# A spiking stage and a linear attention merged into one program by half batches, in a two-layer hybrid kernel

## The reference

```
x = x + attention16(ln(x))       # stage 0, causal, 16 heads, low-rank keys and values
x = x + spiking(ln(x))           # stage 1
x = x + scan(ln(x))              # stage 2, selective scan, with its own rms norm
x = x + spiking(ln(x))           # stage 3, the weights of stage 1
x = x + linear_attention(ln(x))  # stage 4, normalized again, gamma and beta
x = x + experts(ln(x))           # stage 5, 8 experts, all for every token
x = x + attention16b(ln(x))      # stage 6
x = x + experts(ln(x))           # stage 7, the weights of stage 5
```

## Time and profile before

| what | value |
|---|---|
| median of 3 runs | 2260.16 us (2257.64 to 2265.5) |
| the profiled execution | 2259.06 us, of it span 2257.3 |
| mean granted TensorE clock | 0.924 |
| busy: TensorE, VectorE, ScalarE, GpSimd | 1870.5, 1676.5, 1115.6, 1023.6 us |

### The profile page before, as it was taken

The page is one execution under the profiler, slowest core; times in us unless marked ns, Lnnn a source line. Parts: engine busy times, 40 slices in busy tenths (PEclk is TensorE's granted clock), DMA queues, the critical chain, the costliest instruction groups (busy, mean ns, idle before and its releaser), DMA issues.

```text
span 2257.3 us, 32350 instructions
## 1 busy us (share of the span) xinstructions
PE 1870.5 (83%) x12288; PEld 1208.3 (54%) x12288; DVE 1676.5 (74%) x2145; ACT 1115.6 (49%) x1846; POOL 1023.6 (45%) x386
## 2 busy tenths in 40 slices
PE   6988989854888885559999987878887777899999
PEld 5444454343444444446777765555554545577776
DVE  4665555345799995536677779999999999977666
ACT  2344445421634321105555556666676666555554
POOL 3476766511177760110000018878898889700000
PEclk8898999886899997759999999989999999999999
DMA  2112111000200000011000000000000000000000
GB/s 71 29 31 56 29 29 30 1 10 11 38 1 0 1 0 10 5 32 45 27 29 15 15 1 1 1 1 1 2 1 22 9 1 1 29 29 29 15 15 19
DMA packets 35679, 39.12 MB, mean 17 GB/s; under 512 B 5891, under 2 KB 22534, under 8 KB 35526
## 3 DMA queue, kind: packets, MB, share of 16 engines
q1 hardware_dynamic: 34998, 36.01, 6.4%
q10 hardware_dynamic: 528, 1.05, 0.2%
HBM read 21.05 MB, written 1.05 MB: 10 GB/s over the span
## 4 chain that ended last, share of the span: by engine, by line
PE 43%; issue 18%; DVE 18%; POOL 13%; ACT 4%; SPq 2%; DMA 1%; DVEq 0%; POOLq 0%; ACTq 0%; PEldq 0%
PE ps L46 9%; PE ps L48 7%; PE ps L47 7%; DVE negm L2241 6%; POOL AF L698 4%; POOL hc L1332 3%; POOL AF L1332 3%; PE ps L502 2%; PE ps L486 2%; PE ps L527 2%; POOL AR_plain L2051 1%; PE ps L2075 1%; DVE AF L2248 1%; PE ps L2158 1%; PE ps L866 1%
## 5 line engine op out<-in xcount | busy, mean ns | idle before, releaser
L2241 DVE TENSOR_REDUCE negm<-ps 128x64 bf16<-128x1024 f32 x256 | 302.2, 1215 | 14.5 <-PE ps L2149 14.3
L698 POOL TENSOR_TENSOR AF<-AF 128x2048 f32<-128x2048 f32 (+3 forms) x73 | 234.2, 3208 | 154.6 <-ACT AF L638 148.6
L46 PE MATMUL ps<-XH,AR 128*128 128x512 f32 x616 | 257.2, 418 | 36.4 <-DVE AF L907 18.0
L2051 POOL TENSOR_TENSOR AR_plain<-AF 128x2048 f32<-128x2048 f32 x64 | 261.9, 4093 | 35.6 <-ACT AF L2199 34.7
L2207 ACT ACTIVATE AF<-ps 128x1024 f32<-128x1024 f32 x192 | 196.5, 1023 | 144.5 <-PE ps L2158 143.0
L48 PE MATMUL ps<-XH,AR 128*128 128x512 f32 x616 | 247.5, 402 | 0.0
L47 PE MATMUL ps<-XL,AR 128*128 128x512 f32 x616 | 246.9, 401 | 0.0
L2158 PE MATMUL ps<-negm,ident_bf 128*128 128x512 bf16 x512 | 162.4, 400 | 90.0 <-DVE negm L2241 89.9
L638 ACT ACTIVATE AF<-ps 128x512 f32<-128x512 f32 (+1 forms) x304 | 155.5, 576 | 148.3 <-PE ps L489 86.6
L2248 DVE TENSOR_REDUCE AF<-AF 128x128 f32<-128x2048 f32 x96 | 218.6, 2277 | 0.5 <-ACT AF L2207 0.5
L46 PEld LDWEIGHTS ps<-XH,AR 128*128 128x128 f32 x616 | 119.2, 194 | 78.5 <-DVE AF L907 22.5
(11 more groups left out here) (323 smaller groups left out, 4298.0 us busy)
## 6 DMA issues: line engine op xcount, KB each, us to landing
AR<-AR SPq DMA_DIRECT2D x96, 128.0 KB, 2.4
AF<-in_L_ffn_Wg_dram SPq DMA_DIRECT2D x21, 256.0 KB, 2.6
AF<-in_L_ffn_Wu_dram SPq DMA_DIRECT2D x21, 256.0 KB, 3.1
AF<-in_L_ffn_Wd_dram SPq DMA_DIRECT2D x21, 256.0 KB, 3.7
AF<-AF SPq DMA_DIRECT2D x16, 64.0 KB, 2.4
AF<-AR_plain SPq DMA_DIRECT2D x16, 64.0 KB, 2.4
AF<-in_L_attn_a_Wq_dram SPq DMA_DIRECT2D x1, 512.0 KB, 4.2
AF<-in_L_attn_a_Wout_dram SPq DMA_DIRECT2D x1, 512.0 KB, 8.9
```

The lines of the kernel that those rows point to most:

```text
L46: pe.matmul(out, ah, bh, start=start, stop=False)
L698: pool.tensor_tensor(zacc[u % 2][:, :, c0:512], zacc[u % 2][:, :, c0:512], pt[t % 4][:, :, 0:w], ALU.add).then_inc(s0_zp, 1)
L2051: pool.tensor_tensor(p6[m % 3].rearrange("p (j q i) -> p j q i", j=HJ, i=2), e6[m % 4].rearrange("p (j q i) -> p j q i", j=HJ, i=2), w6i[: ...
L2241: dve.tensor_reduce(negm6[:, j % 4, :], bank(2 * (j % 3), 2).rearrange("p (j q i) -> p q j i", j=HJ, i=2), mybir.AxisListType.XY, ALU.max, ...
```

## The change

Four things are done together.

1. **Early weights.** The spiking weights are fetched into `lnt`, a buffer that the norms of stages 2 and 4 use: for stage 1 at the very start of the kernel, for stage 3 once the norm of stage 2 is done. The scan's weights are fetched at the start of stage 1 and transposed ahead of its last `down`, the linear attention's at the start of stage 3, and the first two expert loads stand right behind them on SP.
2. **Heads of stages 1 and 3** by halves and quarters: statistics first, then the first half's norm, its two quarters, and the first up units before the other half.
3. **One program for stages 3 and 4** (`s34_*`). Once the second quarter's spikes are added, batch 0 is normed and its linear attention follows the spiking stage's last quarters in the order written out below. It ends with the norm for the experts of batch 0's two quarters alone.
4. **Guests.** Batch 1's linear attention and its norm for the experts (`s4_end_*`) stand between expert units 0 to 30; the expert units 0 to 31 use batch 0 only. The split of the fourth expert load moves from unit 18 to 20. The scan's buffers and those of stages 3 and 4 lie at other places of the arenas; `s4_*` is cut into one function per step; the addition of the result goes in two parts.

```diff
+        def fc_load(q, k):
+            q.dma_start(FC[k]["fc_raw"], a["L0_ffn_W_fc"]...).then_inc(s1_w, 16)
+            q.dma_start(FC[k]["pj_raw"], a["L0_ffn_W_proj"]).then_inc(s1_w, 16)
         def s1_load(q, s):
             q.wait_ge(x_done, X_AFTER[s])
-            q.dma_start(wfc_raw, ...); q.dma_start(wpj_raw, ...)
+            s2_load_weights(q)
+        def fc_head_pe(pe, s, between=None):
+            k = s // 2
+            fc_weights_pe(pe, k)
+            for i in (0, 1):
+                ln_quarter_pe(pe, s, i, bank(i))
+            fc_up(pe, k, 0)
+            for i in (2, 3):
+                pe.wait_ge(ln_lo, 4 * s + i - 1)
+                ln_quarter_pe(pe, s, i, bank(i - 2))
+            fc_up(pe, k, 1)
+        def fc_norm_dve(dve, link, s):
+            for h in range(2):
+                ln_tiles_stats(dve, link, range(HB * h, HB * h + HB))
+                ln_half_aggr(dve, link, h)
+            ln_tiles_norm(dve, s, range(0, HB))
+        def fc_head_dve(dve, s):
+            for i in (0, 1):
+                ln_quarter_dve(dve, s, i, bank(i))
+            ln_tiles_norm(dve, s, range(HB, NB))
+            fc_squares(dve, k, 0)
+            for i in (2, 3):
+                ln_quarter_dve(dve, s, i, bank(i - 2))
+            fc_squares(dve, k, 1)
...
+            # s1_pe
+            fc_down(pe, 0, 2)
+            s2_weights_pe(pe)
+            fc_down(pe, 0, 3)
...
+        def s34_load(q, s):
+            q.wait_ge(ln_lo, 4 * 2 + 4)
+            fc_load(q, 1)
+            q.wait_ge(x_done, X_AFTER[s])
+            s4_load(q)
+        def s34_pe(pe, s):
+            fc_head_pe(pe, s)
+            s4_weight_pe(pe)
+            fc_down(pe, 1, 0)
+            fc_up(pe, 1, 2)
+            fc_down(pe, 1, 1)
+            fc_up(pe, 1, 3)
+            fc_down(pe, 1, 2)
+            for i in (0, 1):
+                ln_quarter_pe(pe, 4, i, bank(i))
+            fc_down(pe, 1, 3)
+            s4_keys_pe(pe, 0, 6)
+            s4_values_pe(pe, 0, 0)
+            s4_transpose_pe(pe, 0, 6)
+            s4_context_pe(pe, 0, bank(2)[:, 0:P])
+            s4_out_pe(pe, 0, bank(3)[:, 0:P])
+            s4_fold_pe(pe, 0, bank(2)[:, 0:P])
+            pe.wait_ge(s1_yc, 8)
+            for i in (2, 3):
+                ln_quarter_pe(pe, 4, i, bank(2 + i))
+            for p in range(2):
+                s4_result_pe(pe, 0, p, bank(6 + p))
+            for i in (0, 1):
+                ln_quarter_pe(pe, 5, i, bank(i))
+        def s34_dve(dve, link, s):
+            fc_norm_dve(dve, link, s)
+            fc_weights_dve(dve, 1)
+            fc_head_dve(dve, s)
+            fc_spikes(dve, link, 1, 0)
+            fc_squares(dve, 1, 2)
+            fc_spikes(dve, link, 1, 1)
+            dve.wait_ge(x_done, X_AFTER[3] + 2)
+            ln_tiles_stats(dve, link, range(0, HB))
+            ln_half_aggr(dve, link, 0)
+            fc_squares(dve, 1, 3)
+            ln_half_center(dve, link, 4, 0)
+            ln_half_rescale(dve, link, 4, 0)
+            fc_spikes(dve, link, 1, 2)
+            s4_weights_dve(dve)
+            for i in (0, 1):
+                ln_gained_dve(dve, 4, i)
+            fc_spikes(dve, link, 1, 3)
+            s4_max_dve(dve, 0, bank(6, 2))
+            dve.wait_ge(x_done, X_AFTER[4])
+            ln_tiles_stats(dve, link, range(HB, NB))
+            ln_half_aggr(dve, link, 1)
+            s4_sum_dve(dve, link, 0)
+            s4_keys_dve(dve, 0, bank(6, 2))
+            ln_half_center(dve, link, 4, 1)
+            s4_mask_dve(dve, 0, bank(2)[:, 0:P])
+            s4_scale_dve(dve, 0, bank(3)[:, 0:P])
+            ln_half_rescale(dve, link, 4, 1)
+            s4_fold_dve(dve, 0, bank(2)[:, 0:P])
+            for i in (2, 3):
+                ln_gained_dve(dve, 4, i)
+            for p in range(2):
+                s4_add_dve(dve, link, 0, p, bank(6 + p))
+            dve.wait_ge(x_done, X_AFTER[4] + 1)
+            ln_tiles_stats(dve, link, range(0, HB))
+            ln_half_aggr(dve, link, 0)
+            moe_split_dve(dve, 0, 0)
+            ln_tiles_norm(dve, 5, range(0, HB))
+            for i in (0, 1):
+                ln_quarter_dve(dve, 5, i, bank(i))
...
+        END_TR = {27: 2, 28: 3}
+        def s4_end_pe(pe, n):      # called behind down_e(n)
+            if n == 0:
+                s4_keys_pe(pe, 1, 4)
+            if n == 4:
+                s4_values_pe(pe, 1, 4)
+            if n == 7:
+                s4_transpose_pe(pe, 1, 4)
+            if n == 10:
+                s4_context_pe(pe, 1, bank(4)[:, 0:P])
+            if n == 13:
+                s4_out_pe(pe, 1, bank(5)[:, 0:P])
+            if n == 15:
+                s4_fold_pe(pe, 1, bank(4)[:, 0:P])
+            if n in (17, 18):
+                s4_result_pe(pe, 1, n - 17, bank(4 + n - 17))
+            if n in END_TR:
+                ln_quarter_pe(pe, 5, END_TR[n], bank(2 + END_TR[n]))
```

```diff
         def moe_load(q, s):
-            if s == 5:
-                q.wait_ge(x_done, X_AFTER[s])
...
-                if s == 5 and l == 1:
+                if s == 5 and l == 3:
+                    q.wait_ge(x_done, X_AFTER[4])
                     s6_load(q)
```

More of the change, by code:

```diff
@@ new lines, in fc_up @@
+        def fc_up(pe, k, i):
+            for c in range(FF):
+                n = 16 * k + 4 * i + c
+                if i == 0 and c < 2:
+                    pe.wait_ge(s1_flo, k + 1)
+                    pe.wait_ge(s1_fpj, k + 1)
+                pe.wait_ge(ln_lo, 4 * (2 * k + 1) + i + 1)
+                wait(pe, s1_h, n - 1)
+                mm3(pe, bank(2 + n % 2), (FC[k]["hi"][:, P * c:P * c + P], FC[k]["lo"][:, P * c:P * c + P]),
+                    xt(512 * i, 512)).then_inc(s1_z, 1)
@@ new lines, in s4_sum_dve, with s4_transpose_pe @@
+        def s4_sum_dve(dve, link, b):
+            dve.wait_ge(s4_e, b + 1)
+            link(dve.reciprocal(k4r[:, b:b + 1], k4s[:, b:b + 1]))
+        def s4_transpose_pe(pe, b, first):
+            pe.wait_ge(s4_e, b + 1)
+            if b:
+                pe.wait_ge(s4_vc, b + 1)
+            for t in range(LB):
+                ins = pe.transpose(bank(first + t // 4)[:, P * (t % 4):P * (t % 4) + P], k4e[:, P * t:P * t + P],
+                                   ident[:, :])
+            ins.then_inc(s4_kt, 1)
@@ new lines, in s4_fold_dve, with s4_result_pe @@
+        def s4_fold_dve(dve, b, o):
+            dve.wait_ge(s4_cm, 4 * b + 3)
+            dve.tensor_tensor(g4l, o, f32(g4h), ALU.subtract).then_inc(s4_cm, 1)
+        def s4_result_pe(pe, b, p, o):
+            pe.wait_ge(s4_cm, 4 * b + 4)
+            for t in range(4 * p, 4 * p + 4):
+                oo = o[:, P * (t % 4):P * (t % 4) + P]
+                mm3(pe, oo, xt(L * b + P * t, P), (g4h, g4l), stop=False)
+                ins = pe.matmul(oo, ones_row[0:1, :], bout4[0:1, :], start=False, stop=True)
+            ins.then_inc(s4_y, 1)
```

478 lines of the change are left out of this document (289 added, 189 removed).

## The result

The kernel with the change takes 2194.46 us (median of 4 runs, 2187.03 to 2197.44), the kernel before 2259.26 beside it: ratio 0.9703, 95% interval 0.9673 to 0.9734. The prediction was 2198, its range 2184 to 2216. The profiled execution took 2193.45 us, its span 2191.4.

A forecast was written before the change was run, and what follows sets the result against it. It took TensorE to bound the experts and hand-over latency the 161.0 us before them; 2259.1 - 20.6 (A) - 61 (B) + 20 (C) = 2197.5, the median about 1 higher: 2198 us, range 2184 to 2216.

The forecast's parts named there:

- A: First spiking stage to the scan's statistics: early weights and norm by halves give -20.6 us, bounds -16 and -23.
- the old head: Start of the scan stage, from the first of 15 weight fetches to the statistics: goes whole, 16.0 us.
- the clash: First spiking stage's norm: VectorE's two-port and GpSimd's instructions exclude each other; without it the first down block some 2 us earlier.
- B: End of the scan to the first expert matmul: 161.0 us become 100, so -61 us, bounds -52 and -66.
- Rival 5: Second spiking stage and attention: batch 0's attention waits for the whole stage, 20 us of overlap lost, 2218; chance 0.03.
- C: Experts' first 31 units: batch 1's attention and norm as guests cost +20 us, bounds +14 and +30.
- The clump of the exponential: Expert units 2 and 3: two table loads and the exponential, 3.9 us on ScalarE; 4 us TensorE idle for all clumps.
- The result tiles: Batch 1's attention result among the experts: eight tiles at full clock, 8 x 0.94 = 7.5 us.
- rival 4: Experts: TensorE's clock falls to 1.2 GHz throughout the first 32 units, 67 us and guests 7 more, 2272; chance 0.02.
- Rival 2: Experts: each of eleven guest steps empties the two-unit pipeline by about 1.5 us more, guests' cost about 35, 2213; chance 0.17.
- Rival 3: Merged stages warm, result matmuls at 0.94, and guests' clumps hidden: -5 and -5, 2187; chance 0.17.
- Case 1: Experts: guests cost what the forecast says, 2190 to 2208; chance 0.60.

The follow-up runs named there:

- a_late: The kernel after, with the scan's weights fetched, transposed and split at the head of the scan, as before the change: 2207.09 us, 0.9763 of the kernel before.
- a_pool: The kernel after, with GpSimd's memsets of the experts' buffer and the scan's selection matrix held until the norms are done: 2185.47 us.
- The placement runs: Four runs that only move the scan's buffers: two on the kernel before, 2258.27 and 2263.0 us, two on the kernel after, 2196.06 and 2196.65 us.
- b_layout: The kernel before, with only the scan's four float buffers carved first and not last: 2258.27 us, 0.9985 of the kernel before.
- b_shift2: The kernel before, with two unused words ahead of the scan's four float buffers: 2263.0 us, 1.0009 of the kernel before.
- a_exp: The kernel after, with batch 1's keys, maximum and exponential moved ahead of the experts: 2186.25 us, 0.9667 of the kernel before.
- a_shift: The kernel after, with two unused words ahead of all float buffers of the scan: 2196.65 us, 0.9724 of the kernel before.

## Why the prediction was right, step by step

- **A**, -20.6 predicted, -22.3 measured. The removal of the old head (16.0) is confirmed by a_late with 14.0, net of the transposes (13.2 by my sum). The head gained 9.7 and not 7.4. The first square came at 13.4, as predicted with the clash in it; the 2.3 us lie between it and the first down block, for which I had taken' pace of 1.2 us a unit and 2 us of transposes, 10.9 in all, and it took 8.6. From the first down block to the end it lost 3.4, predicted 2.8. The clash still costs 2.1 up to the first square by a_pool, where I had said 2.
- **Scan**, 0 predicted, -4.7 measured. This term was missing. The diff says that buffers lie at other places, and I gave that no cost and no bound. The placement runs show 2.6 of it, and the clock in the stage's head is 1.1.
- **B**, -61 predicted, -62.2 measured (up to 3 us more against the B of b_layout and b_shift2). Every mark of the sum came within 3 us, the early ones 2 to 3 early, the results of batch 0 cold as taken (12.5 against 11.9), the way from there to the first expert matmul 12.1 against 12.2. Rival 5 (no overlap) is refuted: batch 0's attention starts at 40.0 and the last spikes end at 61.2. One bound of the sum is added up wrongly: ten hand-overs of 1 us give -51, not -52.
- **C**, +20 predicted, +26.2 measured. The mechanism held, the size was low within its bounds (14 to 30). The clump of the exponential was taken as 4 and a_exp gives 5.0, with the keys' matmuls of some 1.5 in it. The two table loads stand without a gap, as in the earlier trace rows: the first ends at 942.87 and the exponential starts at 942.88. The result tiles were taken at full clock, 7.5, and took 7.2, so that price was right. What the sum lacked is the clock behind them and at the two waits: four stretches at the lower level, 6.8 us by the estimate above, the two behind the tiles measured at 3. The sum gave the clock in the experts no term, and rival 4 only priced its fall in all of the first 32 units. The fifth, at the end, 1.7 us, is no part of the change. The clash of memsets and norms (1.8 to 4.9 us, the longer case with one of these stretches in it) was not in the sum either, although I had priced the same clash in A: I moved the memsets to about unit 28, only asked what waits for them on SP, and did not see that the norms stand at 27 and 28. Against this, units 8 to 19 took only 1.7 for some 3.4 us of guests: TensorE was not as full there as 97% made it look.
- **Rival 2** (stalls, part C 35): its mechanism is real in two clumps, at 2.61 and 2.88 us of idle, but not in eleven. **Rival 3** (warm and tight, 2187): not in the change's profiled execution; but a_late shows half of its first part, four of the eight result tiles and part of a fifth at 0.90 us, B 2.7 us shorter in unedited code. **Rival 4** (clock falls in all of the first 32 units): it falls in four stretches (949 to 952, 989 to 993, 996 to 1000, 1020 to 1024), some 14 us in all, not for a run of units, and units 31 to 64 keep 77.1. Case 1 is what came: units 0 to 30 are 24.4 us longer, under the 30 that would have made me wrong, and two more table loads are there (8 for 6).
- The median, 3.5 us under the forecast: the terms missed -4.7 (scan), -2.9 (A and B), +6.2 (C), and the start, -2.0, where executions of the same code differ by 8. That the scan's -4.7 and C's +6.2, from unrelated causes, cancel for the most part is luck.

## What to carry to other kernels

Work of another batch is worth putting into a full engine's stream when the alternative is a block of hand-overs at the lower clock: 26.7 against 48.7 us here, and some 35 by estimate for a block in a better order. But first fill the holes of the block that remains: keys, exponential and values cost nothing there and 7.6 us as guests (units 3 to 7, 19.8 against 12.2). When an instruction of GpSimd moves, ask which VectorE instruction it now stands beside, not only who waits for it; and when buffers move, compare how the inputs of two-input GpSimd instructions stand to 16 bytes.

## What the runs showed of the hardware

- GpSimd's `tensor_tensor` of 128x1024 float32 takes 2.38 to 2.40 us with inputs that start alike modulo 16 bytes and 2.00 us with inputs 8 bytes apart, six kernels of six. Whether it is GpSimd's own reads or their meeting with VectorE's, which works beside it, stays open; no run took VectorE away.
- The granted clock fell to its lower level with TensorE busy 2.00 of 2.00 us, on 512-column matmuls right behind four tiles of 128 columns with one-row float32 products between them (990 to 992 above). In the same unchanged code it falls in one execution and not in another: units 112 to 127, which hold tiles of 128 columns with a 64-row product behind each, took 48.6 to 48.7, 50.2 or 51.8 to 51.9 us with none, one or two such stretches, and the B of unedited code moved by 3 us (a_late against after; b_layout and b_shift2 against before). Differences of up to 3.3 us between single traces are therefore no evidence for an edit.
- Units 28 to 30 with the memset clash took 8.8 to 8.9 or 11.4 to 12.0 us, the latter always with a stretch at the lower clock. In the longer case TensorE's wait is 2.88 us and the matmul behind it 0.80 us long; it was 0.50 in a_shift, behind a wait of 1.71.
- A one-row float32 product of 128 columns costs 0.9 us at 1.2 GHz, against 0.21 for one of 128 rows in the rounded format.
